# Score products of attention: two stacked products of 128 rows against three of 64 rows, one bank in each half of the array

## The reference

```python
q = jnp.einsum('bnd,hde->bhne', query, Wq) * scale
k = jnp.einsum('bmd,hde->bhme', query, Wk)
v = jnp.einsum('bmd,hde->bhme', query, Wv)
logits = jnp.einsum('bhne,bhme->bhnm', q, k)
attn = jax.nn.softmax(logits, axis=-1)
out = jnp.einsum('bhnm,bhme->bnhe', attn, v)
```

## Time and profile before

| | |
|---|---|
| median of 3 runs | 2236.65 us (2232.92 to 2238.29) |
| span of the profiled execution | 2233.3 us |
| its time as a whole | not given apart from its span |
| attention's slots | about 49 to 1767 us |
| TensorE matmul busy | 2113.3 us, 95% |
| TensorE weight load busy | 1835.2 us, 82% |
| VectorE busy | 1795.7 us, 80% |
| ScalarE busy | 1484.9 us, 66% |
| GpSimd busy | 285.1 us, 13% |
| mean granted clock of TensorE | 0.974 of 2.4 GHz |

### The profile page before, as it was taken

How to read it: one execution, slowest core, us unless ns; L and a number is a source line. 1 busy time by engine, 2 the same in 40 slices (tenths; PEclk the granted TensorE clock), 3 DMA queues, 4 the chain that set the end, 5 groups by cost and what they waited for, 6 DMA issues and landing times. The chain is left out here.

```text
span 2233.3 us, 39878 instructions
## 1 busy us (share of the span) xinstructions
PE 2113.3 (95%) x12888; PEld 1835.2 (82%) x12888; DVE 1795.7 (80%) x2870; ACT 1484.9 (66%) x2703; POOL 285.1 (13%) x258
## 2 busy tenths in 40 slices
PE   5999999999999999999999999999999888848996
PEld 4888888888888888888888888888888687848886
DVE  3888888888888888888888888888889566656775
ACT  3777777777777777777777777777778535324453
POOL 1000000100000000000000000000000222324664
PEclk8999999999999999999999999999999999958999
DMA  8434343434343434344343434343423464213341
GB/s 282 142 76 128 76 127 75 140 84 135 87 132 88 132 87 125 97 105 122 80 127 75 127 75 127 75 127 75 127 66 97 130 214 127 92 41 117 123 142 48
DMA packets 159018, 248.59 MB, mean 111 GB/s; under 512 B 61676, under 2 KB 121196, under 8 KB 153964
## 3 DMA queue, kind: packets, MB, share of 16 engines
q1 hardware_dynamic: 155884, 239.33, 38.0%
q0 software_dynamic: 3072, 8.46, 1.1%
HBM read 93.27 MB, written 33.62 MB: 57 GB/s over the span
## 5 line engine op out<-in xcount | busy, mean ns | idle before, releaser
L607 DVE TENSOR_TENSOR pT_lo<-pT_ps,pT_hi 128x512 fp32r<-128x512 f32 x1024 | 655.3, 681 | 22.8 <-ACT pT_hi L536 17.3
L569 DVE TENSOR_REDUCE neg_max<-scores 128x1 f32<-128x1024 f32 x512 | 623.3, 1218 | 35.8 <-PE scores L410 35.8
L536 ACT ACTIVATE pT_hi<-pT_ps 128x512 fp32r<-128x512 f32 x1024 | 559.6, 600 | 112.9 <-PE pT_ps L425 109.8
L509 ACT ACTIVATE probs<-scores,neg_max 128x1024 f32<-128x1024 f32 x512 | 573.7, 1121 | 22.7 <-DVE neg_max L569 22.7
L425 PEld LDWEIGHTS pT_ps<-ident,probs 128*128 128x128 f32 x4096 | 475.3, 140 | 82.2 <-DVE pT_lo L607 8.0
L425 PE MATMUL pT_ps<-ident,probs 128*128 128x128 f32 x4096 | 537.7, 274 | 2.6 <-DVE pT_lo L607 2.5
L444 PE MATMUL av_ps<-pT_hi,v_st 128*128 128x512 f32 x1024 | 445.7, 435 | 0.7 <-DVE pT_lo L607 0.7
L409 PE MATMUL scores<-k_hh,q_st 128*128 128x512 f32 x1024 | 412.0, 402 | 3.5 <-ACT probs L509 2.0
L445 PE MATMUL av_ps<-pT_lo,v_st 128*128 128x512 f32 x1024 | 402.5, 393 | 0.0
L410 PE MATMUL scores<-k_ll,q_st 128*128 128x512 f32 x1024 | 402.4, 393 | 0.0
L409 PEld LDWEIGHTS scores<-k_hh,q_st 128*128 128x128 f32 x1024 | 192.8, 188 | 39.2 <-ACT probs L509 2.7
(11 more groups left out here) (195 smaller groups left out, 2581.9 us busy)
## 6 DMA issues: line engine op xcount, KB each, us to landing
k_hh<-qk_hi SPq DMA_DIRECT2D x128, 256.0 KB, 4.7
k_ll<-qk_lo SPq DMA_DIRECT2D x128, 256.0 KB, 4.8
xT<-xT_parts SPq DMA_DIRECT2D x15, 2048.0 KB, 10.4
q_st<-qk_hi SPq DMA_DIRECT2D x64, 256.0 KB, 4.4
q_st<-qk_lo SPq DMA_DIRECT2D x64, 256.0 KB, 4.9
v_st<-v_st SPq DMA_DIRECT2D x16, 1024.0 KB, 5.7
o_tokens<-o_out SPq DMA_DIRECT2D x32, 512.0 KB, 3.2
w_raw<-in_L_ffn_W_dram SPq DMA_DIRECT2D x16, 1024.0 KB, 6.0
```

Of the source, the lines that this page charges most:

```text
L509: act.activation(probs[:, tt % 2, :], scores[tt % 2][:, :], ACT.Exp, bias=neg_max[:, tt % 4:tt % 4 + 1], accum_out=row_sum[:, tt % IT_T:tt ...
L536: act.activation(pT_hi[:, (tt // CH) % 2, half * CH:(half + 1) * CH, (tt % CH) * P:(tt % CH + 1) * P], pT_ps[half][:, :, :], ACT.Copy).the ...
L569: dve.tensor_reduce(neg_max[:, tt % 4:tt % 4 + 1], scores[tt % 2][:, :], AX.X, ALU.max, negate=True).then_inc(max_ready, 1)
L607: dve.tensor_tensor(pT_lo[where], pT_ps[half][:, :, :], pT_hi[where].bitcast(F32), ALU.subtract).then_inc(pT_lo_done, 1)
```

## The change

Each score tile is now made by six products of 64 rows, three for each bank. Bank 0 (keys 0 to 511) is computed in the lower half of the rows, partitions 0 to 63, and bank 1 (keys 512 to 1023) in the upper half; in program order the two halves alternate. The three products are high x high, high x low and low x high; low x low is left out. Both halves now need q high and q low, so a second buffer, `q_sw`, holds q with its halves exchanged. `k_hh` and `k_ll` keep only one bank's keys in each half, and are half as long. The lay-out takes 16 copies for a pair (`ASM`) in place of 12. `oT` has one place in place of two, and ScalarE's copy into it waits for the fold of the chunk before it. The x^T of the fourth batch uses `q_sw` where it used `k_hh`.

```diff
@@ -83,7 +83,7 @@
     CHUNKS = NT // CH
     T_PAIRS = TILES // 2
     GROUPS = B * T_PAIRS
-    ASM = 12
+    ASM = 16
     assert 2 * E == P and HP == 8 and SCALE == 0.125
     ident, ident_zeroed, ident_ready, _ = const
 
@@ -108,14 +108,15 @@
         wv_hi = sb("wv_hi", [P, KC, 4 * E], F32R)
         wv_lo = sb("wv_lo", [P, KC, 4 * E], F32R)
         q_st = sb("q_st", [P, 2, 2, N], F32R)
-        k_hh = sb("k_hh", [P, 2, 2, N], F32R)
-        k_ll = sb("k_ll", [P, 2, 2, N], F32R)
+        q_sw = sb("q_sw", [P, 2, 2, N], F32R)
+        k_hh = sb("k_hh", [P, 2, 2, BANK], F32R)
+        k_ll = sb("k_ll", [P, 2, 2, BANK], F32R)
 
         v_st = sb("v_st", [P, 3, HP, 2, HILO, E], F32R)
         probs = sb("probs", [P, 2, N])
         pT_hi = sb("pT_hi", [P, 2, HP, BANK], F32R)
         pT_lo = sb("pT_lo", [P, 2, HP, BANK], F32R)
-        oT = sb("oT", [P, 2, BANK])
+        oT = sb("oT", [P, BANK])
         o_sum = sb("o_sum", [P, CH, E])
         o_out = sb("o_out", [P, 2, TILES, 2 * E])
         neg_max = sb("neg_max", [P, 4])
@@ -137,7 +138,7 @@
             if b == 0:
                 return xT[:, 0], xT[:, 1]
             if b == 3:
-                return q_st[:, 1], k_hh[:, 1]
+                return q_st[:, 1], q_sw[:, 1]
             both = (pT_lo[:, b - 1].rearrange("p m n -> p (m n)")
                     .rearrange("p (a k n) -> p a k n", a=HILO, k=KC))
             return both[:, 0], both[:, 1]
@@ -249,15 +250,18 @@
             def lay_out_q(par):
                 for h in range(2):
                     rows = slice(h * E, (h + 1) * E)
-                    for dst, src in ((q_st[lo, par, h], qk_hi[rows, 0]), (q_st[hi, par, h], qk_lo[rows, 0])):
+                    for dst, src in ((q_st[lo, par, h], qk_hi[rows, 0]), (q_st[hi, par, h], qk_lo[rows, 0]),
+                                     (q_sw[lo, par, h], qk_lo[rows, 0]), (q_sw[hi, par, h], qk_hi[rows, 0])):
                         sp.dma_start(dst.bitcast(F32), src.bitcast(F32)).then_inc(qk_laid, 16)
 
             def lay_out_k(par):
                 for h in range(2):
                     rows = slice(h * E, (h + 1) * E)
-                    for buf, src in ((k_hh, qk_hi[rows, 1]), (k_ll, qk_lo[rows, 1])):
-                        for half in (lo, hi):
-                            sp.dma_start(buf[half, par, h].bitcast(F32), src.bitcast(F32)).then_inc(qk_laid, 16)
+                    for half, cols in ((lo, slice(0, BANK)), (hi, slice(BANK, N))):
+                        sp.dma_start(k_hh[half, par, h].bitcast(F32), qk_hi[rows, 1, cols].bitcast(F32)
+                                     ).then_inc(qk_laid, 16)
+                        sp.dma_start(k_ll[half, par, h].bitcast(F32), qk_lo[rows, 1, cols].bitcast(F32)
+                                     ).then_inc(qk_laid, 16)
 
             def store_o(g, par, batch, head):
                 wait_then(sp, o_done, 4 * (g + 1), const[3])
@@ -403,11 +407,16 @@
                 if u == 0:
                     wait(pe, qk_laid, 16 * ASM * ((T // PAIR_T if isinstance(T, int) else 2 * it + pair) + 1))
                 wait(pe, probs_ready, T - 1)
-                q = q_st[:, par, h, j * P:(j + 1) * P]
-                for c in range(N // BANK):
-                    cols = slice(c * BANK, (c + 1) * BANK)
-                    pe.matmul(scores[tt % 2][:, cols], q, k_hh[:, par, h, cols], start=True, stop=False)
-                    last = pe.matmul(scores[tt % 2][:, cols], q, k_ll[:, par, h, cols], start=False, stop=True)
+                rows = slice(j * P, (j + 1) * P)
+                lower, upper = slice(0, E), slice(E, P)
+                c0, c1 = slice(0, BANK), slice(BANK, N)
+                out = scores[tt % 2]
+                pe.matmul(out[:, c0], q_st[lower, par, h, rows], k_hh[lower, par, h, :], start=True, stop=False)
+                pe.matmul(out[:, c1], q_sw[upper, par, h, rows], k_hh[upper, par, h, :], start=True, stop=False)
+                pe.matmul(out[:, c0], q_st[lower, par, h, rows], k_ll[lower, par, h, :], start=False, stop=False)
+                pe.matmul(out[:, c1], q_sw[upper, par, h, rows], k_ll[upper, par, h, :], start=False, stop=False)
+                pe.matmul(out[:, c0], q_sw[lower, par, h, rows], k_hh[lower, par, h, :], start=False, stop=True)
+                last = pe.matmul(out[:, c1], q_st[upper, par, h, rows], k_hh[upper, par, h, :], start=False, stop=True)
                 last.then_inc(scores_ready, 1)
 
             def slot(it, tt):
@@ -462,7 +471,7 @@
                     misc_free(f, done)
                     for m in range(CH):
                         last = pe.transpose(misc_ps[:, m * P:(m + 1) * P],
-                                            oT[:, (tt // CH) % 2, m * P:(m + 1) * P], ident[:, :])
+                                            oT[:, m * P:(m + 1) * P], ident[:, :])
                     last.then_inc(fold_ready, 1)
 
             pe.wait_ge(ident_ready, 1)
@@ -520,8 +529,8 @@
                 if tt % CH == 0 and (not first or tt >= 2 * CH) and exists(it, tt, -2 * CH):
                     c = it * (IT_T // CH) + tt // CH - 2
                     wait(act, av_ready, c + 1)
-                    wait(act, fold_ready, c - 1)
-                    act.activation(oT[:, (tt // CH) % 2, :], av_ps[:, :], ACT.Copy).then_inc(oT_done, 1)
+                    wait(act, fold_ready, c)
+                    act.activation(oT[:, :], av_ps[:, :], ACT.Copy).then_inc(oT_done, 1)
                 if isinstance(it, int) and it == ITS - 1 and tt == IT_T - CH:
                     act.wait_ge(bite_ready, bites_to(1, it))
                     early.split_wp_high(act)
```

## The result

The changed kernel takes 2298.88 us (median of 4 runs, 2296.84 to 2299.96) against 2236.77 us before (median of 4 runs): ratio 1.028, 95% interval 1.026 to 1.029. It is **62 us slower**, where 95 us faster was forecast.

A forecast was written before the change was run, and what follows sets the result against it. TensorE was taken to set the pace, VectorE close behind. 108 us gained on paired score products less 13 us lost to VectorE gave 95, so 2236.65 went to 2142 us; range 2125 to 2406.

The forecast's parts named there:

- What bounds the kernel: In attention TensorE's matmuls set the pace, busy 2113 of 2233 us; VectorE follows at 87% in a middle stretch.
- The pair: Two half-height score matmuls run at once; a tile's six cost 0.71 us, not 0.92, gaining 108 us in all.
- The crossing: Switching between full- and half-height products, entering and leaving each score tile, 1024 times: taken near nothing, bounds 0 to 0.27 us.
- the point from which it decides: Cost of one switch between full and half height at which the whole change turns to a loss: 0.105 us.
- my upper bound: Most one switch of height could cost: a 0.16 us matmul tail plus a 0.11 us uncovered load, together 0.27 us.
- The first rival: Each switch of height at a score tile drains TensorE: 56 to 169 us slower, 2293 to 2406 us; chance 0.30.
- VectorE: In four-slot attention groups without bites, VectorE becomes the bound and keeps back some 13 us of the gain.
- The lay-out and `oT`: Sixteen copies per pair of heads and one `oT` buffer cost nothing; late copies bounded at 32 us.
- draining crossings: Each switch of height at a score tile waits for TensorE to empty: 2293 to 2406 us; chance 0.30.
- The halves don't overlap: The six half-height score matmuls of a tile run one after another: 236 us slower, 2473 us; chance 0.14.

The follow-up runs named there:

- the kernel with crossings alone: The kernel before with its four score products a tile cut to the lower 64 rows, lay-out and buffers unchanged: 2413.58 us, ratio 1.079.

## Why the prediction was wrong, point by point

**What bounds the kernel**: right for the kernels before and after. TensorE paces both, and what made its slot longer came through in full (177 us in the kernel with crossings alone, 346 with serial halves). What made it shorter came through only in part (63 of 118 us), since VectorE takes over.

**The pair**: right, and slightly better than taken. I priced three pairs at 0.71 us, between 0.69 and a floor of 0.72 from six loads. The loads of a pair run side by side as the matmuls do (1042.70 and 1042.71), so that floor isn't there; a pair costs 0.23., which I cited for loads and matmuls, show matmuls alone.

**The crossing: the step that failed.** I put the two crossings of a tile at nothing, because the change from transposes to products shows no emptying. That row is no measure of it: both run at full height. Measured is 0.17 us a crossing, 0.34 a tile, which turns a gain of 118 us into a loss of 56. The bounds, 0 to 0.27 us, held, and so did the point from which it decides, 0.105. Both parts of my upper bound are there on the way in, one at half its size: of the tail of 0.16 us about 0.08 is waited for, and the bare load costs the 0.11 of the earlier trace rows. On the way out to the transposes it is 0.10 and 0.05. That the tail and the load are what these pieces consist of is read from the timelines; the price of a crossing is what the experiments show.

The first rival named this mechanism and gave 2293 to 2406 us; the measured 2299 is near its lower end. That is partly luck: this end is a whole tail at each crossing and no load, 2 x 0.16 = 0.32 us on pairs of 0.71, where the timeline has 0.34 us of other parts on pairs of 0.69. "TensorEngine Tiling (Array Packing)", "Tiling Modes", of the Trainium skill states that such a switch drains TensorE. The trace of the changed kernel agrees in part: the load comes 0.36 us late and doesn't run ahead over the crossing, but the first pair starts at 1042.70, 0.08 us before the last product's 1042.39 + 0.39.

**VectorE: mis-sized.** I put 13 us on it, from whole groups of four slots without bites. With three full-height products it kept back 118 - 63 = 55 us. A fold puts VectorE behind, and it has only 2.5 - 2.33 = 0.17 us a slot to catch up in, so the wait recurs in slots that I had counted as free. With free crossings and this the forecast would have been about 2173 us. In the changed kernel as it ran neither the 13 us nor the 55 play a part, since the crossings make its slots longer (2.85 us) than those before (2.72 at their commonest) and leave VectorE the time.

**The lay-out and `oT`**: right, nothing (2173.14 against 2173.17 us).

**The rivals**: draining crossings, at 0.30, came true. "The halves don't overlap", at 0.14, is out: with serial halves the kernel takes 346 us more. The range of 2125 to 2406 held the time, because it spanned the gain and the loss; the sign was wrong.

Do the experiments point to a faster kernel? Those with fewer full-height products are faster, but leave terms of the score out. With the same terms the half-height form would have to be entered less often. An estimate: two tiles for one entry would save, of a slot of 2.85 us, 0.17 of the 0.34; the net against the kernel before is then 0.23 - 0.17 = 0.06 us a slot, 31 us at best, and VectorE and the two score buffers stand in the way. It wasn't tried.

## What to carry to other kernels

Half-height products that alternate between the halves cost half, and the engine finds the overlap by itself; but each entry into the form and each exit costs, here 0.17 us, three quarters of a matmul of 512 columns. Count the crossings before counting the matmuls saved: one saved matmul for two crossings loses. And where another engine is at 87%, take away a matmul without putting anything in its place first, to see how much there is to win: here 63 us of 118. And a wait in the table is not yet a wait for the engine named: if every tile has it at the same length, as the 0.36 us here, look for one cause behind both names.

## What the runs showed of the hardware

- Two half-height matmuls of 512 columns in the two halves start 0.01 us apart and cost 0.23 us together, and their loads start 0.01 us apart too; 2644.5 - 2298.9 = 346 us is what the overlap is worth over 1536 matmuls.
- A crossing between full and half height costs 0.17 us (177 us over 1024 of them). On the way in 0.11 of it is a load that no longer runs ahead. It is much the same into the form (0.19) and out of it (0.15 into transposes, 0.20 into products).
- TensorE starts a matmul of the free half ahead of two that stand before it in the program: 1001.60 against 1001.92 and 1002.15, and so in 430 of 430 tiles.
- Sixteen copies of 3 MB in all take SP a little longer to issue than twelve, but less than their number says: 962.13 to 977.4 us in one lay-out of the changed kernel (15.2 us), against 1039.03 to 1051.97 before (12.9 us), where 16 / 12 would give 17.3. With the time from issue to landing of a `k_ll` copy, 2.4 in place of 4.8 us, both end after some 17.6 us.
